# Router logits from extra columns of the v and projection matmuls, in place of a transposed x1

## The reference, cut to what matters

```python
x = layernorm(x + attn(x, W_key, W_query, W_value, W_proj))      # x1
# attn ends with: einsum('bto,po->btp', out, W_proj) * 256 ** -0.5
scores = softmax(einsum('bsd,ed->bse', x, router_w))             # 8 experts
gate_vals, sel_idx = top_k(swapaxes(scores, 1, 2), 129)
# per expert: gelu(tokens @ w1 + b1) @ w2 + b2, times gate, added at sel_idx
x = layernorm(x + moe(x))
```

## Time and profile before

| | |
|---|---|
| median of 3 runs | 985.91 us (981.85 to 986.39) |
| profiled execution | 987.11 us |
| its span | 985.4 us |
| TensorE busy | 853.1 us (87%), 6044 matmul passes |
| VectorE busy | 655.1 us (66%) |
| ScalarE busy | 524.4 us (53%) |
| GpSimd busy | 523.8 us (53%) |
| granted TensorE clock | 0.929 of full on the mean |

### The profile page before, as it was taken

The page is one execution under the profiler, slowest core; times in us unless marked ns, Lnnn a source line. Parts: engine busy times, 40 slices in busy tenths (PEclk is TensorE's granted clock), DMA queues, the critical chain, the costliest instruction groups (busy, mean ns, idle before and its releaser), DMA issues. The chain is left out here.

```text
span 985.4 us, 17316 instructions
## 1 busy us (share of the span) xinstructions
PE 853.1 (87%) x6044; PEld 647.9 (66%) x6044; DVE 655.1 (66%) x1957; ACT 524.4 (53%) x994; POOL 523.8 (53%) x621
## 2 busy tenths in 40 slices
PE   4568899999999999888669599998989999898990
PEld 3334455564646454434359589998989989898990
DVE  4457677888787778889938974646464644646454
ACT  3026666657666656555518245554555546455555
POOL 5336565556565563323545527657474655747443
PEclk9669999999999999988859799998999989999995
DMA  4987667777776758310142314344242342512248
GB/s 132 161 156 120 118 120 140 141 140 141 134 136 103 132 104 145 128 41 2 44 150 76 112 23 65 77 92 118 47 116 36 79 92 33 135 29 38 39 125 249
DMA packets 90166, 100.26 MB, mean 102 GB/s; under 512 B 9056, under 2 KB 83552, under 8 KB 89952
## 3 DMA queue, kind: packets, MB, share of 16 engines
q1 hardware_dynamic: 72288, 77.66, 37.8%
q0 software_dynamic: 12800, 16.92, 10.2%
q10 hardware_dynamic: 4992, 4.59, 1.4%
HBM read 65.12 MB, written 33.62 MB: 100 GB/s over the span
## 5 line engine op out<-in xcount | busy, mean ns | idle before, releaser
L497 DVE CUSTOM_DVE_ANT_0 n_ps<-n_ps,tri 128x512 f32<-128x512 f32 (+3 forms) x512 | 237.2, 520 | 73.6 <-PE n_ps L622 72.3
L1055 DVE TENSOR_TENSOR h_lo<-g,h_hi 128x384 fp32r<-128x384 f32 (+1 forms) x184 | 138.1, 759 | 129.2 <-ACT h_hi L991 120.8
L411 ACT ACTIVATE pt<-st_ps 128x512 f32<-128x512 f32 x320 | 181.8, 603 | 77.1 <-PE st_ps L607 70.0
L1131 PE MATMUL y_ps<-w_parts,h_hi 128*128 128x256 f32 (+1 forms) x1152 | 212.4, 279 | 0.0
L986 ACT ACTIVATE g<-h_ps,b 128x384 f32<-128x384 f32 (+1 forms) x192 | 104.2, 543 | 195.5 <-PE h_ps L1117 159.6
L1117 PE MATMUL h_ps<-tt_hi,w_parts 128*128 128x384 f32 (+1 forms) x768 | 179.2, 338 | 30.6 <-issue 20.0
L359 POOL TENSOR_SCALAR_AFFINE_SELECT pt<-pt 128x256 f32<-128x256 f32 (+1 forms) x320 | 111.3, 361 | 147.4 <-ACT pt L411 145.9
L1131 PEld LDWEIGHTS y_ps<-w_parts,h_hi 128*128 128x128 f32 (+1 forms) x1152 | 171.8, 177 | 3.3 <-ACT h_hi L991 0.2
L958 POOL DMA_INDIRECT acc<-y,tok_no x64 | 103.1, 1611 | 117.1 <-DVE y L1069 106.4
L1131 PE MATMUL y_ps<-w_parts,h_lo 128*128 128x256 f32 (+1 forms) x576 | 160.6, 279 | 0.0
L1117 PEld LDWEIGHTS h_ps<-tt_hi,w_parts 128*128 128x128 f32 x768 | 134.1, 200 | 32.9 <-issue 31.7
(11 more groups left out here) (149 smaller groups left out, 1152.4 us busy)
## 6 DMA issues: line engine op xcount, KB each, us to landing
w_parts<-part_d SPq DMA_DIRECT2D x192, 128.0 KB, 6.6
w_raw<-in_w SPq DMA_DIRECT2D x16, 1024.0 KB
part_d<-w_raw SPq DMA_DIRECT2D x96, 128.0 KB, 7.4
w_raw<-in_xt SPq DMA_DIRECT2D x8, 512.0 KB, 4.5
res<-in_x SPq DMA_DIRECT2D x8, 512.0 KB, 10.8
x<-res SPq DMA_DIRECT2D x8, 512.0 KB, 6.6
acc<-res SPq DMA_DIRECT2D x8, 512.0 KB, 8.2
fin<-acc SPq DMA_DIRECT2D x4, 512.0 KB, 4.1
```

The source lines that it names most:

```text
L411: nc.scalar.activation(pt[:, slot % PT_RING, n % UP, :], st_ps[at % ST_RING][:, :], ACT.Exp, scale=S_SCALE).then_inc(exp_done, 1)
L497: ins = nc.vector.tensor_tensor_reduce(out=src[:, h, :], in0=src[:, h, :], in1=mask, scale=-1.0, scalar=-BIG_NEG, op0=ALU.add, op1=ALU.min ...
L1055: nc.vector.tensor_tensor(h_lo[:, q % 2, n, 0:cols], g[:, at % G_RING, 0:cols], h_hi[:, q % 2, n, 0:cols].bitcast(F32), ALU.subtract).then ...
L1131: ins = nc.tensor.matmul(y_ps[at % Y_RING][0:rows, 0:C], x[:, q % 2, m, toks], w[e % 2][:, m, :], start=i == 0, stop=i == len(terms) - 1)
```

## The change

Eight columns with the centred router weights stand behind the 256 columns of v's weights, and eight with W_proj's product with them behind the projection's. ScalarE copies x's share of the logits from the v tile into `scores`; VectorE adds the projection's share there, and after rstd is known multiplies by it. `x1t`, its copies, its SBUF tile and the logit matmuls go. A tile of v and of the projection is now one token block of 264 columns, so there are four of each. `centre` and `fold` prepare the weights once, during the first sequences' start; the projection weights are loaded behind the second x load, together with a second copy in the other order (`wpn`), which lies in `o_nat` for the time.

```diff
 STAGES
-    (1, 9, 'proj', -1, 0),
+    (1, 8, 'proj', -1, 0),
     (1, 9, 'proj', -1, 1),
+    (2, 0, 'proj', -1, 2),
+    (2, 1, 'proj', -1, 3),
     (2, 5, 'x1', -1, 0),
     (2, 5, 'v', 2, 0),
-    (2, 7, 'v', 2, 1),
-    (2, 9, 'x1t', -1, 0),
+    (2, 6, 'v', 2, 1),
+    (2, 7, 'logit', -1, 0),
+    (2, 7, 'v', 2, 2),
+    (2, 8, 'v', 2, 3),
-    (3, 1, 'x1t', -1, 1),
+    (3, 2, 'score', -1, 0),
-    (3, 4, 'logit', -1, 0),
-    (3, 9, 'score', -1, 0),
 steps(), at (-2, 0, 0)
-  ("qk", 0), ("qk", 1), ("stack", 0), ("v", 0), ("qk", 2), ("qk", 3), ("v", 1)
+  ("qk", 0), ("qk", 1), ("stack", 0), ("centre", 0), ("qk", 2), ("qk", 3), ("v", 0), ("v", 1), ("v", 2), ("v", 3)
+  if (i, g, k) == (-1, 2, 0): yield "fold", 0, 0
 sync
-  sp.dma_start(wp[...]) and rw at the start, then_inc(wp_in, 16) each
+  sp.dma_start(rw[...]).then_inc(rw_in, 16)
+  # behind load_xt(1): wpn, then wp
   elif stage == "res":
-    sp.wait_ge(act_ready, act_no[("x1t", b - 2, 1)] + 1)
 scalar
   elif stage == "v":
-    for t in range(2):
-        ins = nc.scalar.activation(vaug[:, b % 3, 2 * n + t, :, 0:D], src[:, t, :, :], ACT.Copy)
+    nc.scalar.activation(vaug[:, b % 3, n, :, 0:D], src, ACT.Copy)
+    nc.scalar.activation(scores[:, n, b, :], ps[:, C:C + E], ACT.Copy).then_inc(act_free, 1)
-  elif stage == "x1t": (copy to x1t)
   elif stage == "logit":
-    act.wait_ge(dve_free, dve_no[(stage, b, n)] + 1)
+    act.wait_ge(lg_ready, b + 1)
 vector
+  elif stage == "centre": rw -= mean (from PSUM); w_hi, w_lo columns 3C..3C+E from rw
+  elif stage == "fold": wp[:, :, C:C + E] = av_ps
   elif stage == "proj":
-    scalar_tensor_tensor of 512 columns, two bn_stats, two bn_aggr
+    nc.vector.scalar_tensor_tensor(out=row, in0=ps[:, 0:C], scalar=O_SCALE, in1=row, ...)
+    nc.vector.scalar_tensor_tensor(out=u, in0=ps[:, C:C + E], scalar=O_SCALE, in1=u, ...).then_inc(dve_free, 1)
+    link(nc.vector.bn_stats(stats[:, n, :], row))
+    if n == TT - 1: four bn_aggr
   elif stage == "logit":
-    src = ps[:, 0:TT * E]
+    u = scores[:, :, b, :]
     max over u, lg = u - max
+    nc.vector.tensor_tensor(lg, lg, rstd (broadcast), ALU.mult).then_inc(lg_ready, 1)
 tensor
   elif stage == "v":
+    toks = slice(n * P, (n + 1) * P)
+    ins = nc.tensor.matmul(ps[:, 0:C + E], x[:, k, toks], w[:, k, 2 * C:3 * C + E], ...)
+  elif stage == "centre": 2 matmuls of rw with a matrix of 1/C into av_ps
+  elif stage == "fold": 4 matmuls of wpn with rw into av_ps
   elif stage == "proj":
+    ins = nc.tensor.matmul(ps[:, 0:C + E], o_t[:, k, toks], wp[:, k, :], ...)
-  elif stage == "x1t": 4 transposes per tile
-  elif stage == "logit": 8 matmuls
```

More of the change, by code:

```diff
@@ L93 @@
 AV_PLACES = (4, 5, 6, 7)
-BY_ACT = ("qk", "v", "nm", "ot", "x1t")
-BY_DVE = ("onorm", "proj", "logit", "pick", "picked")
+BY_ACT = ("qk", "v", "nm", "ot")
+BY_DVE = ("onorm", "proj", "pick", "picked")
 def steps():
@@ L153, in weight_parts, with attention @@
     return both[:, 0, :, :], both[:, 1, :, :]
-def attention(nc, ctx, xt_d, x_d, wqkv_d, wp_d, rw_d, x1_d, acc_d, ident, scores, chosen, w1_d, w2_d, ahead):
+def attention(nc, ctx, xt_d, x_d, wqkv_d, wp_d, wpn_d, rw_d, x1_d, acc_d, ident, scores, chosen, w1_d, w2_d, ahead):
     def sb(name, shape, dt):
@@ L220, in attention @@
     wp_in = sem("wp_in")
+    wpn_in = sem("wpn_in")
+    rw_in = sem("rw_in")
+    rw_mean = sem("rw_mean")
+    rw_split = sem("rw_split")
+    rw_fold = sem("rw_fold")
+    wp_ready = sem("wp_ready")
     w_split = sem("w_split")
@@ L249, in attention @@
     x1_out = sem("x1_out")
+    lg_ready = sem("lg_ready")
     lexp = sem("lexp")
@@ L531, in _ @@
                     dve.wait_ge(res_in[b % 2], 16 * (b // 2 + 1))
-                rows = res[:, b % 2, 2 * n:2 * n + 2, :].rearrange("p t c -> p (t c)")
-                nc.vector.scalar_tensor_tensor(out=rows, in0=ps[:, :], scalar=O_SCALE, in1=rows,
+                row, u = res[:, b % 2, n, :], scores[:, n, b, :]
+                nc.vector.scalar_tensor_tensor(out=row, in0=ps[:, 0:C], scalar=O_SCALE, in1=row, op0=ALU.mult, op1=ALU.add).then_inc(dve_step, 1)
+                made[0] += 1
+                nc.vector.scalar_tensor_tensor(out=u, in0=ps[:, C:C + E], scalar=O_SCALE, in1=u,
                                                op0=ALU.mult, op1=ALU.add).then_inc(dve_free, 1)
[L535 to L548, removed]
+                dve.wait_ge(dve_step, made[0])
+                link(nc.vector.bn_stats(stats[:, n, :], row))
+                if n == TT - 1:
+                    for t in range(TT):
+                        nc.vector.bn_aggr(mv[:, t, :], stats[:, t, :]).then_inc(dve_step, 1)
+                    made[0] += TT
+                    dve.wait_ge(dve_step, made[0])
                     nc.vector.tensor_scalar_add(ve[:, :], mv[:, :, 1], EPS).then_inc(var_ready, 1)
@@ L656, in _ @@
             elif stage == "v":
[L657 to L663 removed]
+                if b == 0 and n == 0:
+                    pe.wait_ge(rw_split, 1)
+                toks = slice(n * P, (n + 1) * P)
+                for at, (w, x) in enumerate(((w_hi, xt_hi), (w_hi, xt_lo), (w_lo, xt_hi))):
+                    for k in range(KC):
+                        ins = nc.tensor.matmul(ps[:, 0:C + E], x[:, k, toks], w[:, k, 2 * C:3 * C + E],
+                                               start=at + k == 0, stop=at == 2 and k == KC - 1)
+                ins.then_inc(act_ready, 1)
+            elif stage == "centre":
+                pe.wait_ge(rw_mean, 1)
+                pe.wait_ge(rw_in, 16)
+                for k in range(KC):
+                    ins = nc.tensor.matmul(av_ps[:, 0:E], mean_of[:, :], rw[:, k, :], start=k == 0, stop=k == KC - 1)
+                ins.then_inc(rw_mean, 1)
+            elif stage == "fold":
+                pe.wait_ge(wpn_in, 16)
+                pe.wait_ge(rw_split, 1)
+                for m in range(KC):
+                    for k in range(KC):
+                        ins = nc.tensor.matmul(av_ps[:, m * E:(m + 1) * E], wpn[:, k, m * P:(m + 1) * P], rw[:, k, :],
+                                               start=k == 0, stop=k == KC - 1)
+                ins.then_inc(rw_fold, 1)
             elif stage == "nm":
@@ L697, in _ @@
                 nc.tensor.transpose(ps[:, early:2 * early], best[:, 0:P], ident[0:early, 0:early]).then_inc(dve_ready, 1)
-            elif stage == "logit":
-                pe.wait_ge(act_free, act_no[("x1t", b, 1)] + 1)
-                for t in range(TT):
-                    for k in range(KC):
-                        ins = nc.tensor.matmul(ps[:, t * E:(t + 1) * E], x1t[:, k, t * P:(t + 1) * P], rw[:, k, :],
-                                               start=k == 0, stop=k == KC - 1)
-                ins.then_inc(dve_ready, 1)
 LEFT = B
@@ L1168, in build @@
         with ExitStack() as ctx:
-            attention(nc, ctx, xt_d, x_d, wqkv_d, wp_d, rw_d, x1_d, acc_d, ident, scores, chosen, w1_d, w2_d, ahead)
+            attention(nc, ctx, xt_d, x_d, wqkv_d, wp_d, wpn_d, rw_d, x1_d, acc_d, ident, scores, chosen, w1_d, w2_d, ahead)
         with ExitStack() as ctx:
```

80 lines of the change are left out of this document (42 added, 38 removed).

## The result

| | before | after |
|---|---|---|
| median of 19 runs each | 985.21 us (981.85 to 988.96) | 994.02 us (985.51 to 997.72) |
| ratio | | 1.0084, 95% interval 1.0069 to 1.0100 |
| profiled execution, its span | 987.11 us, 985.4 | 996.38 us, 994.6 |
| TensorE busy, mean granted clock | 853.1 us, 0.929 | 848.8 us, 0.916 |

The account below looks back on a forecast made before the run. TensorE looked like the bound, with a second path through gapless VectorE; the seventh period was VectorE's. Terms -2.5 - 1.1 + 1.2 - 1.5 - 3.3 = -7.2 gave 979.9, on the median 978.7 us, range 965 to 987.

Parts of the forecast that it names:

- ScalarE's wait at (2,7): Rival, chance 0.09: TensorE's 1.75 us standing at (3,0) is added to each period and lets the clock fall; 997 us.
- Clock: Granted clock fell in two of five periods, 1.45 us each; one fall taken as gone, -1.5 us, bounds -2.9 and +4.4.
- It then lacks the logits' 1.81: TensorE, 1.07 us late at (3,4), no longer has the logit passes' 1.81 us: 0.74 us earlier at (3,5).
- the removed burst: TensorE's transposes and logit passes, done just before the clock fell; their removal was to take one of two falls.
- ScalarE's wait: At (2,7) the exp waits for VectorE's logits with v's copies and score exps queued behind; TensorE stands 1.75 us at (3,0).
- VectorE's moved operations: Logit work moved to (2,7) and score to (3,2), in VectorE's gapless stretch: maxima at (3,4) come 0.66 us later.
- Projection and statistics: VectorE's projection work +1.1 us a period, covered by its 2.95 us wait before x1; TensorE's added columns 0.2 us.
- The transposes' 0.9 us: Eight transposes removed from TensorE each period, about 0.9 us, worth nothing since VectorE and ScalarE end later there.
- Sixth period: From 384 us, no v copies behind the exp, TensorE held only by maxima: -1.1 us, bounds 0 and -2.5.
- Seventh: Period bound by VectorE, busy 43.3 of 47.3 us, which gets 1.3 us more: +1.2 us, bounds 0 and +1.5.
- Tail: After the last x1 the block ends with the stores at 507.0 instead of 510.3: -3.3 us, bounds -4 and -2.
- Start: Later split, weight loads, centring and folding hidden behind DMA waits before the first sequences: 0 us, bounds -0.5 and +1.5.

Follow-up runs that it names:

- e3: Changed kernel with the logits' softmax steps back at (3,4) and (3,9) and nmt's three DMAs issued by SP instead of ScalarE: 965.31 us, 0.9806 of before.
- e6: Changed kernel with TensorE passes that nobody reads filling its stands at (3,0), (3,7) and (3,8): 984.74 us, 0.9977 of before.
- e2: Changed kernel with nmt's three DMAs issued by SP instead of ScalarE: 974.97 us, 0.9889 of before.
- e11: Changed kernel with only ScalarE's exp of the logits (3,4) and the score (3,9) late, VectorE's three logit operations left at (2,7): 985.62 us.
- e1: Changed kernel with the logits' softmax steps back at (3,4) and the score at (3,9): 978.13 us, 0.9927 of before.
- e10: e3 with the score at (3,7) and the pick of the first six sequences begun two places earlier: 976.91 us, 0.9907 of before.
- e7: Changed kernel with softmax steps at (3,4) and score at (3,9) for the seventh period's sequence only: 990.55 us, 1.0041 of before.

## Why the prediction was wrong

The forecast was 978.7 us, the range 965 to 987, with 0.09 for slower. The time came near where the rival "ScalarE's wait at (2,7)" put it, 997 us. It has the right reason, TensorE's stand and the falls behind it, but that the sum came so near is in part luck: it charged 1.25 us a period for standing, where the fall-free period grew by about 0.35, and took too little for the clock and for the seventh period, and it had nothing on ScalarE's DMA issue.

- **The step that failed most: "Clock", one of two falls gone, -1.5 us.** It became +6.4 in four periods alone (9.3 against 2.9 us, by the estimate under e3). The upper bound of +4.4 took one fall of 1.45 us a period as the most; there were up to two, and some twice as long. I had seen that TensorE would stand at (3,0), and counted the removed burst instead. e6 shows that the stands were it: fill the stands, and the kernel is as fast as before.
- **"It then lacks the logits' 1.81": the overlap was missed.** TensorE's passes hid ScalarE's issue of three DMAs, 1.94 us beside them. I had not read it, because it isn't counted as busy and no wait of TensorE's in that period ended with it. In the half after (3,4) the changed kernel gains 0.4 us without falls (23.04 to 22.63); with the issue on SP the same half takes 21.05 (e2). So a period became about 0.35 us longer, 52.3, not 0.5 shorter, 51.4.
- **ScalarE's wait: right in place and size** (2.15 us waited, 2 or more forecast; TensorE 1.19, 1.75 forecast). From (1,4) to (3,4) the half period grew by 0.75 us, 1.3 forecast. Without falls it and VectorE's early steps cost 0.4 a period, 0.07 where the DMA issue is gone: it stands where TensorE would soon wait for maxima. What it did was to the clock.
- **VectorE's moved operations: right.** 0.66 us later maxima forecast, 0.49 by e11 against e1. But the forecast took a duration for constant that depends on what GpSimd does beside it (e10).
- **Projection and statistics: right on VectorE**, 0.42 and 0.155 us each, and it still waited 2.92 us before x1. On TensorE the columns cost more busy time than the 0.2 us taken: projection 4.4 for 3.7 us, v 5.3 for 5.0. The transposes' 0.9 us are gone and e3's half from (1,4) to (3,4) is still 0.21 longer; 0.25 was forecast. Whether VectorE or the wider passes take up the transposes' time no run here parts.
- **Sixth period:** -0.1 for -1.1; the gain is there (44.7 in e3) and went into a fall of 3.4 us lost at 424 and the same two stands.
- **Seventh: +1.2 forecast, +3.9 measured.** I had added VectorE's work and not asked what stands before the logits in its queue there: two rounds, and behind ScalarE's wait for them TensorE. e7 takes all of it back. About 1.9 us of it is the conversion at 501.26, shifted beside a GpSimd operation: before, changed and in e7, x1 ends 11.3 to 11.4 us behind the end of the conversion, so its length passes through.
- **Tail: right**, -3.1 for -3.3: the block ends 4.9 us after x1, by a store. Start: -1.3 for 0. The first period took +2.0, with the fall at 161, which the kernel before lacks there.

## What to carry to other kernels

When work comes off the leading engine, list what the other engines do beside it, issue of DMAs included, for that is what ends last next; here, moving three DMA starts to an idle queue was worth 0.4% before the change and 1.3 to 1.9% after it (e3 against e1, e2 against the changed kernel). A short wait placed where it seems covered can still cost through the clock: count the stands, not only their sum, and read the granted clock beside the periods. Keep small steps that nobody waits for out of the stretch where their engine is gapless, and out of another engine's queue until their input is surely there.

## What the runs showed of the hardware

- **The clock fell behind short stands.** From 220 to 275 us TensorE was idle for no longer than 1.19 us at a time, busy 93% of the time, and the granted clock still was at 1.2 GHz for 6.8 us. A fall of 1.7 us lost cost 1.2 (e2) to 1.45 us (before). In the changed kernel's halves after (3,4), a fall twice as long cost 1.7 us more than a single one (25.20 for 23.50). Passes that nobody reads kept the clock at 2.4 GHz (e6).
- **A small VectorE operation sometimes ended only when a GpSimd one beside it did.** The conversion of 48x136 took 2.16 us and ended with GpSimd's operation (503.42 and 503.34), 0.22 alone; in e11 the product of 128x32 took 4.20 us in the same way, in e10 1.52. The maxima and searches of the pick beside the same GpSimd operations kept their 0.68 us. The Trainium skill, "SBUF — State Buffer", section "SBUF: two separate sides", has this as a port pair which VectorE, with two inputs in SBUF or in a fast mode, and GpSimd hold in turn for a whole instruction. The traces agree for the product, which has two inputs in SBUF; the conversion has one, and whether it runs in a fast mode no run here shows.
- **Three DMA starts held ScalarE 1.95 us**, 0.65 each, and appear in no busy time.
